# Nine one-hot quads shared between VectorE and ScalarE in the setup, and an earlier codebook request, in a one-core attention and codebook-FFN kernel

## The reference, cut to what matters

```
p = tanh(|phz|) * exp(1j * angle(phz));  prog = p ** arange(L)         # the turns
conv = causal convolution of silu(layernorm(h)) with prog, plus lc * prog * p
Wg, Wu, Wd = codebook[idx_gate], codebook[idx_up], codebook[idx_down]  # dequantized
y = silu(x @ Wg.T) * (x @ Wu.T) @ Wd.T
```

## Time and profile before

| | us |
|---|---|
| three runs: median (lowest to highest) | 1321.85 (1320.96 to 1324.58) |
| the profiled execution, its time | 1320.63 |
| its span in the profile | 1318.8 |
| busy: TensorE, VectorE, ScalarE | 1246.8, 1052.7, 272.3 |
| the setup, up to the first instruction of the attention stage on TensorE | 86.6 |

### The profile page before, as it was taken

One profiled execution on the slowest core, in us unless ns is written; L12 is line 12 of the kernel. 1 busy time (PEld: TensorE's weight loads), 2 busy tenths in 40 slices (PEclk: granted clock), 3 DMA queues, 4 the chain that ended last, 5 costly groups with the idle time before them and its releaser, 6 DMA issues.

```text
span 1318.8 us, 20711 instructions
## 1 busy us (share of the span) xinstructions
PE 1246.8 (95%) x7362; PEld 925.8 (70%) x7362; DVE 1052.7 (80%) x2356; ACT 272.3 (21%) x461; POOL 845.4 (64%) x815
## 2 busy tenths in 40 slices
PE   6868999978999999999999999999999999999988
PEld 4534445434777777777777777777777777789866
DVE  3998888868888778888778888778888778888735
ACT  2326666665101000000000000000001000100115
POOL 3666666666676667776667776666776666777710
PEclk8978999986999999999999999999999999999989
DMA  9222222210333323343323433323433323434203
GB/s 233 34 70 53 47 51 51 51 12 9 91 91 86 75 62 86 88 97 84 76 63 80 97 90 85 73 62 80 92 93 84 68 67 78 97 72 88 52 1 128
DMA packets 94619, 98.79 MB, mean 75 GB/s; under 512 B 48109, under 2 KB 52981, under 8 KB 94518
## 3 DMA queue, kind: packets, MB, share of 16 engines
q1 hardware_dynamic: 64884, 89.16, 22.6%
q0 software_dynamic: 25600, 3.33, 8.5%
q10 hardware_dynamic: 4034, 4.98, 1.3%
HBM read 92.50 MB, written 4.90 MB: 74 GB/s over the span
## 4 chain that ended last, share of the span: by engine, by line
PE 78%; DVE 12%; issue 4%; ACT 3%; POOL 1%; DMA 1%; SPq 1%; POOLq 0%; DVEq 0%; ACTq 0%
PE cand L655 41%; PE bank L655 36%; DVE one_hot L1038 3%; DVE work L1022 2%; DVE work L1286 2%; POOL stage_down L400 1%; DVE chosen L1056 1%; ACT L431 1%; DMA book_in<-in_L_ffn_codebook 1%; PE cand L827 1%; DVE small L1022 1%; DVE h L1248 1%; DVE x L1022 0%; SPq L298 0%; ACT work L431 0%
## 5 line engine op out<-in xcount | busy, mean ns | idle before, releaser
L400 POOL DMA_INDIRECT stage_down<-in_L_ffn_codebook,idx_down x688 | 723.4, 1051 | 350.5 <-issue 168.7
L655 PE MATMUL cand<-one_hot,book 128*128 128x512 f32 (+1 forms) x2592 | 660.4, 397 | 15.3 <-DVE one_hot L1038 15.3
L1038 DVE TENSOR_SCALAR one_hot<-bc,low_of 128x512 fp32r<-128x512 uint16 (+1 forms) x1296 | 541.0, 479 | 98.9 <-PE cand L655 96.0
L655 PEld LDWEIGHTS cand<-one_hot,book 128*128 128x128 f32 x2592 | 485.3, 190 | 146.9 <-DVE one_hot L1038 23.2
L655 PE MATMUL bank<-x1t_hi,w 128*128 128x512 f32 (+1 forms) x704 | 244.4, 403 | 0.0
L1056 DVE SCALAR_TENSOR_TENSOR chosen<-bc,high_of,cand 128x512 f32<-128x512 uint16 (+1 forms) x324 | 234.8, 725 | 3.7 <-PE cand L655 3.7
L387 POOL DMA_INDIRECT stage_gate<-in_L_ffn_codebook,idx_gate x112 | 120.0, 1071 | 61.4 <-issue 25.8
L655 PEld LDWEIGHTS bank<-x1t_hi,w 128*128 128x128 f32 (+1 forms) x704 | 129.9, 186 | 37.0 <-issue 7.3
L655 PE MATMUL bank<-x1t_lo,w 128*128 128x512 f32 (+1 forms) x352 | 141.8, 403 | 0.0
L464 ACT ACTIVATE w<-bank 128x128 fp32r<-128x128 f32 (+1 forms) x88 | 24.0, 273 | 402.7 <-PE bank L655 387.2
L1022 DVE TENSOR_TENSOR x<-x,bank 128x512 f32<-128x512 f32 x84 | 57.3, 682 | 52.5 <-PE bank L655 52.2
(11 more groups left out here) (176 smaller groups left out, 784.6 us busy)
## 6 DMA issues: line engine op xcount, KB each, us to landing
bc<-index_parts SPq DMA_DIRECT2D x292, 256.0 KB, 3.2
stage_down<-in_L_ffn_codebook,idx_down POOLq DMA_INDIRECT x688, 2.7
bc<-index_parts_rest SPq DMA_DIRECT2D x32, 192.0 KB, 3.1
x<-in_L_attn_x ACTq DMA_DIRECT2D x4, 1024.0 KB, 10.9
out_x<-x SPq DMA_DIRECT2D x16, 256.0 KB, 2.0
stage_gate<-in_L_ffn_codebook,idx_gate POOLq DMA_INDIRECT x112, 2.9
index_parts<-parts_t SPq DMA_DIRECT2D x20, 32.0 KB, 2.3
w_in<-in_L_attn_W ACTq DMA_DIRECT2D x2, 256.0 KB
```

The source lines that it names most:

```text
L400: pool.indirect_dma_start(stage_down[k % RING][:, q, j * CS:(j + 1) * CS], None, a["L0_ffn_codebook"], bass.IndirectOffsetOnAxis(ap=idx_do ...
L655: return pe.matmul(dst, lhs, rhs, start=start, stop=stop)
L1038: done = v.tensor_scalar(one_hot[quad % 2][:, q, 0:nw], bc[quad % BCS][:, 0:nw], low_of[:, q:q + 1], None, ALU.is_equal)
```

## The change

- ScalarE makes the third and fourth one-hot tile of quads 0 to 8: `Abs(low - column)` and then `Relu(1 - that)`. VectorE makes the first and second. `candidates` waits for ScalarE's tiles only ahead of the third matmul.
- The conversion of the index parts of tiles 1 to 10 to float, and the four `mix` matrices, go from VectorE to ScalarE.
- `unit` runs after every third doubling only.
- On SP's queue, the codebook's two requests stand ahead of `parts_out(0)`; on VectorE, the wait for the codebook and its split stand ahead of the wait for the turned rows of parameters.

```diff
             # sync
-            parts_out(0)
             for half in range(2):
                 sp.dma_start(book_in[...], ...).then_inc(s["book_in"], 16)
+            parts_out(0)
             for quad in range(BCS):
                 spread_parts(quad)
             # scalar
+            def hots(quad):
+                place = one_hot[quad % 2]
+                act.wait_ge(s[f"bc_in{quad % BCS}"], 16 * (quad // BCS + 1))
+                if quad >= 2:
+                    act.wait_ge(s["candidates"], quad - 1)
+                for n in range(2):
+                    act.activation(place[:, LT - 2 + n, :], bc[quad % BCS][:, 0:4 * P], ACT.Abs, bias=less_low[:, n:n + 1]
+                                   ).then_inc(s["distance_made"], 1)
+                for n in range(2):
+                    act.wait_ge(s["distance_made"], 2 * quad + n + 1)
+                    act.activation(place[:, LT - 2 + n, :], place[:, LT - 2 + n, :].bitcast(F32), ACT.Relu, bias=one[:, 0:1], scale=-1.0
+                                   ).then_inc(s["act_hot_made"], 1)
...
             act.activation(small[:, 8, :], small[:, 7, :], ACT.Sqrt).then_inc(s["phase_sqrt"], 1)
+            act.wait_ge(s["hot_biases"], 2)
+            hots(0)
             act.wait_ge(s["b1_made"], 1)
             keep_h(0, bank[2])
+            hots(1)
             for t, b in ((4, 0), (5, 1), (6, 2), (7, 0)):
                 keep_x(t, bank[b])
             keep_h(1, bank[1])
+            for l in range(L):
+                done = act.activation(mix[:, l, :], centre[:, :], ACT.Copy, scale=cols[:, l, SC_LIN:SC_LIN + 1])
+            done.then_inc(s["mix_made"], 1)
+            hots(2)
             act.wait_ge(s["mag_made"], 1)
             act.activation(cols[:, :, DECAY], small[:, 9, :], ACT.Tanh).then_inc(s["phase_tanh"], 1)
             for t, b in ((8, 2), (9, 0), (10, 1), (11, 2)):
                 keep_x(t, bank[b])
             keep_h(2, bank[0])
+            hots(3)
             for t, b in ((12, 1), (13, 2), (14, 0), (15, 1)):
                 keep_x(t, bank[b])
             keep_h(3, bank[2])
+            act.wait_ge(s["idx_cut"], 2)
+            act.activation(idx_low[:, 1:TILES, :], low_i[:, 1:TILES, :], ACT.Copy)
+            act.activation(idx_high[:, 1:TILES, :], high_i[:, 1:TILES, :], ACT.Copy).then_inc(s["idx_split"], 1)
+            hots(4)
             act.wait_ge(s["eps_made"], 1)
             square1(0)
             for k in range(1, TILES):
                 keep_parts(k, bank[(k - 1) % 3])
                 if k == 5:
                     keep_picked(0)
+                if k in (2, 4, 8):
+                    hots({2: 5, 4: 6, 8: 7}[k])
+            hots(EARLY)
             # tensor, in candidates(quad)
+                        if quad <= EARLY and m == 0 and q >= LT - 2:
+                            pe.wait_ge(s["act_hot_made"], 2 * quad + q - (LT - 2) + 1)
             # vector
-                for q in range(LT):
+                for q in range(LT - 2 if quad <= EARLY else LT):
...
+            v.memset(one[:, :], 1.0).then_inc(s["hot_biases"], 1)
+            v.tensor_scalar(less_low[:, :], iota_low[:, LT - 2:LT], -1.0, None, ALU.mult).then_inc(s["hot_biases"], 1)
...
+            v.wait_ge(s["book_in"], 32)          # with the split of the codebook, moved up from behind b1_made
+            for q in range(LT):
+                link(v.tensor_copy(book[0]...)); tt(book[1]..., ALU.subtract)
             v.wait_ge(s["rows_turned"], 1)
...
-                unit(k + 1, S[10], S[11])
+                if k % 3 == 2:
+                    unit(k + 1, S[10], S[11])
...
-            v.tensor_copy(idx_low[:, 1:TILES, :], low_i[:, 1:TILES, :])
-            v.tensor_copy(idx_high[:, 1:TILES, :], high_i[:, 1:TILES, :]).then_inc(s["idx_split"], 1)
...
-                v.tensor_scalar(mix[:, l, :], centre[:, :], cols[:, l, SC_LIN:SC_LIN + 1], None, ALU.mult)
```

More of the change, by code:

```diff
@@ L171, in build @@
         high_of = sb("high_of", [P, 1])
+        less_low = sb("less_low", [P, 2])
+        one = sb("one", [P, 1])
         one_hot = [sb(f"one_hot{b}", [P, LT, 4 * P], F32R) for b in range(2)]
@@ L253, in build @@
         sem_names = """consts_made masks_made iotas_made eps_made means_made centre_made
-            first_index_in index_in index_down_in index_gate_in idx_cleared first_split idx_split rows_in x_in0 x_in1 x_in2 x_in3 w_in bout_in book_in
+            first_index_in index_in index_down_in index_gate_in idx_cleared first_split idx_cut idx_split rows_in x_in0 x_in1 x_in2 x_in3 w_in bout_in book_in
             parts_turned parts_kept parts_out0 parts_out1 parts_out2 turned_x x_kept turned_w w_kept rows_turned cols_made sums_made b1_made bout_sum bout_made
-            h_sum h_begun phase_sqrt phase_tanh q_made mag_made link layer_made book_made
+            h_sum h_begun phase_sqrt phase_tanh q_made mag_made link mix_made layer_made book_made
             sq1_made var1 rs1_made normed1 silu_made turned_back scanned damped rotated state_kept mixed h_mid
@@ L259, in build @@
             attn_out x_added stats_made aggregated rstd_made shift_made x1_made x1_turned x1_hi x1_lo
-            bc_in0 bc_in1 bc_in2 bc_in3 bc_in4 one_hot_made candidates chosen_made summed picked_hi picked_lo
+            bc_in0 bc_in1 bc_in2 bc_in3 bc_in4 hot_biases distance_made act_hot_made one_hot_made candidates chosen_made summed picked_hi picked_lo
             gate_in down_in0 down_in1 down_in2 turned_down w_hi w_lo gate_made up_made gate_silu product act_hi_made act_lo_made
@@ L817, in _ @@
             pe.wait_ge(s["layer_made"], 1)
+            pe.wait_ge(s["mix_made"], 1)
             pe.wait_ge(s["means_made"], 1)
@@ L1083, in _ @@
             v.tensor_copy(high_of[:, :], iota_m[:, :])
+            v.wait_ge(s["book_in"], 32)
+            for q in range(LT):
+                link(v.tensor_copy(book[0][:, q, :].rearrange("p (e h) -> p h e", e=CS), book_in[:, :, q, :]))
+                tt(book[1][:, q, :].rearrange("p (e h) -> p h e", e=CS), book_in[:, :, q, :],
+                   book[0][:, q, :].rearrange("p (e h) -> p h e", e=CS).bitcast(F32), ALU.subtract).then_inc(s["book_made"], 1)
             v.wait_ge(s["rows_turned"], 1)
@@ L1113, in _ @@
             done.then_inc(s["b1_made"], 1)
[L1114 to L1118, removed]
             one_hots(0)
@@ L1155, in double @@
                     tt(tabq[:, :, new], ta, tb, ALU.add)
+                squared = (S[10], S[11]) if k % 3 == 2 else (cosp[:, :, k + 1], sinp[:, :, k + 1])
                 tt(S[0], cosp[:, :, k], cosp[:, :, k], ALU.mult)
                 tt(S[1], sinp[:, :, k], sinp[:, :, k], ALU.mult)
-                link(v.scalar_tensor_tensor(S[11], cosp[:, :, k], 2.0, sinp[:, :, k], ALU.mult, ALU.mult))
-                link(tt(S[10], S[0], S[1], ALU.subtract))
-                unit(k + 1, S[10], S[11])
+                link(v.scalar_tensor_tensor(squared[1], cosp[:, :, k], 2.0, sinp[:, :, k], ALU.mult, ALU.mult))
+                link(tt(squared[0], S[0], S[1], ALU.subtract))
+                if k % 3 == 2:
+                    unit(k + 1, S[10], S[11])
             double(0)
@@ L1166, in _ @@
             v.wait_ge(s["index_in"], 64)
-            link(v.tensor_scalar(by_quad(low_i, 1, TILES), strided(raw, 1, TILES), LOW - 1, None, ALU.bitwise_and))
-            v.tensor_copy(idx_low[:, 1:TILES, :], low_i[:, 1:TILES, :])
-            link(v.tensor_scalar(by_quad(high_i, 1, TILES), strided(raw, 1, TILES), LOW.bit_length() - 1, None, ALU.logical_shift_right))
-            v.tensor_copy(idx_high[:, 1:TILES, :], high_i[:, 1:TILES, :]).then_inc(s["idx_split"], 1)
+            v.tensor_scalar(by_quad(low_i, 1, TILES), strided(raw, 1, TILES), LOW - 1, None, ALU.bitwise_and).then_inc(s["idx_cut"], 1)
+            v.tensor_scalar(by_quad(high_i, 1, TILES), strided(raw, 1, TILES), LOW.bit_length() - 1, None, ALU.logical_shift_right
+                            ).then_inc(s["idx_cut"], 1)
             double(2)
```

## The result

The changed kernel took 1335.9 us, median of 6 runs (1331.57 to 1339.37), against 1321.08 for the one before (6 runs, 1319.97 to 1324.58): 14.8 us more, a ratio of 1.012 (95% interval 1.0101 to 1.014). The forecast was 1334, slower.

What follows compares the result with a forecast made beforehand. VectorE looked like the bound, but queue order and handovers decide: late parameters, ScalarE's pieces and late broadcasts move the opening root from 89.4 to 102.3, +12.9 on 1320.6, 1333.5 profiled, median 1334; range 1325 to 1341.

Steps and rivals of the forecast that it cites:

- The codebook: SP's queue: requested 1.3 us earlier, landing 0 to 1.3 sooner, taken as 0.6, at 25.0; `bc` 0 at 29.5 to 30.
- The late parameters: VectorE takes the parameter rows only after the codebook's split, 27.4; `h_in(0)` starts at 32.6, first turns of x 8.5 us later.
- ScalarE's pieces: One-hot pieces 2.45 us a quad, both casts 2.45, four `mix` 1.1; ScalarE gets 25.6 us for VectorE's 9.9.
- The clock: TensorE's `h_in(2)`, its candidates and the next round's follow gaps over 3 us: 0.5 us added a round for lower clock.
- The tiles: Index tiles: first `keep_parts` at 74.4; behind SP's output issues `bc` 7 lands 87.9, `bc` 8 97.9; root ends 102.3.
- Setup and total: Opening root ends at 102.3 against 89.4, +12.9; nothing later takes the shift back; median forecast 1334.
- VectorE's relief is the gain: First rival: VectorE was the bound and ScalarE's share hides wholly; gain of some 6 us, 1316; 7 in 100.
- the gains and losses cancel: Second rival: codebook 1.3 sooner, pieces 2.06, no lower clock, tiles and `bc` issued sooner: 1324 to 1326; 10 in 100.
- the third rival: ScalarE costs more: pieces at 3.3 us a quad, +7, or half clock in rounds two to four, some 4; 15 in 100.
- Table loads: ScalarE: one 1.28 us load counted, after `hots(8)`, without the 1.38 drain; abs and relu outside active tables: up to nine more.

Runs made afterwards that it cites:

- second profile: Another profiled execution of the changed kernel, with a span of 1333.7 us; the first profiled execution took 1339.37.
- experiment 1: Changed kernel with the codebook's wait and split back behind `b1_made` on VectorE, SP's order staying changed: 1374.16 us, ratio 1.0072 to the kernel before.
- sixth: Changed kernel with the codebook's part undone on both SP and VectorE, all else as changed: 1326.99 us, ratio 1.0066 to the kernel before.
- seventh experiment: Kernel before with only the rarer renormalization (`unit` after every third doubling): 1317.8 us against 1319.12, ratio 0.999.
- second group: Group of follow-up runs with the kernel before on the same chip: kernel before 1319.12 us, changed kernel again 1334.69.

## Why the prediction was right, step by step

| step | before | forecast | changed | codebook undone |
|---|---|---|---|---|
| `h_in(0)` starts | 22.22 | 32.6 | 33.83 | 22.45 |
| `h_in(1)` | 34.42 | 43.3 | 44.31 | 35.24 |
| `h_in(2)` | 42.58 | 54.8 | 56.21 | 46.90 |
| `h_in(3)` | 50.73 | 64.1 | 67.38 | 58.52 |
| first tile kept | 56.55 | 74.4 | 77.00 | 68.13 |
| opening root ends | 89.4 | 102.3 | 106.3 | 97.0 |

VectorE's first scan in the attention stage, before and after, for the step behind the setup:

```profile
92.88 1.28 DVE L1286 TENSOR_TENSOR_SCAN work<-cols,work 128x512 f32<-128x512 f32 x1
```

```profile
109.14 1.28 DVE L1326 TENSOR_TENSOR_SCAN work<-cols,work 128x512 f32<-128x512 f32 x1
```

- **The codebook.** It landed at 25.2, and the forecast said 25.0: of 1.3 us sooner in the queue 0.4 arrived, and in the second profile (25.62 against 25.61) nothing. SP came back at 21.0, not 19.8, `bc` was asked for at 26.05 and was there by 30.44, hidden as forecast.
- **The late parameters.** The mechanism was right and is confirmed by undoing it (7.7 us in time, 9.2 at the root; this takes back SP's order too). From the rows to `h_in(0)` it took 6.0 us, not 5.2: after ten idle microseconds TensorE's granted clock was 0.50 at 22 to 30 us, and the stretch with its many narrow matmuls took 1.1 us longer than before, where I had added 0.3.
- **ScalarE's pieces.** 2.45 us a quad, 1.26 a cast and 1.27 for four `mix` were forecast within 0.2 us. That the one-hot pieces lose in the rounds is shown by leaving them out (about 7 us at the root).
- **The clock**, the term that was too small. I had 0.5 us in each of two rounds; it was 2.3 in one and nothing in the other. That it is the clock, and that it fell in the 3.2 us gap ahead of the turn (0.51 at 54 to 56 us), is shown by filling this gap, which brought the 2.3 back. Shorter gaps can go either way: the fourth round's, 0.5 and 0.8 us, left the projection at 3.70, those of 0.8 and 2.0 us in experiment 1 stood before one of 5.40.
- **The tiles.** From the first kept tile to the root I had 27.9 us, it took 29.3: `bc` of quad 7 landed 3.7 us after its issue where I had 3.4, and from its landing to the end of tile 10 it took 6.0 us (90.93 to 96.88) where I had 5.3: the candidates of quad 7, 4.1 us long at a granted clock of 0.50, ended 2.6 us behind ScalarE's pieces where I had 2.1.
- **Setup and total.** The setup was lengthened by 16.9 us, 4.0 more than the sum. The medians differ by 14.8, so some 2 us came back later, where I had seen nothing that would take the shift back. The scans of the attention stage, one in each of its 16 items, show how it goes on. The first of them is 16.3 us late (92.88 before, 109.14 after), so 0.6 us came back at once, and all 16 are 16.2 to 16.3 late, in the second profile 16.3 to 16.4: the stage hands the shift through. The second profile was 15.9 us late at the first candidates beside the FFN (337.12 against 321.22) and 14.9 at the end. The first was 17.7 late there and 18.8 at the end, so executions of the same kernel part behind the attention stage, and what takes or gives there stays open. The closeness of 1334 to 1335.9 owes something to luck: two errors of opposite sign, 4.0 too little in the setup and some 2 us that came back.
- **The rivals.** That VectorE's relief is the gain falls with the sixth and seventh experiment: even alone on the kernel before, 5.8 us less work gave 2.1 at the root and, in time, nothing that the interval tells from zero. That the gains and losses cancel did not occur. Of the third rival a part did: one `h_in` at the lower clock, not three, and pieces at the price that I had taken.
- **Table loads.** On ScalarE the load ahead of the root begins 0.01 us after the piece before it (102.94 + 1.32, 104.27), and the root 0.02 us after the load (105.57): no drain of the kind that the Trainium skill, "ScalarE: Activation LUTs", section "What ACT_TABLE_LOAD costs", states is to be seen. The prediction says that it counted one load, but its walk has a second one on the path, with the Tanh up to 52.8. Two drains of the page's 1.38 us would have made the sum +15.7, an estimate that is nearer to the measured 16.9 than mine, yet the rows leave no room for the second either: pieces until 52.35, load at 52.37, Tanh at 53.67. The rule of the same page, section "Table sets: the hidden batching unit", that abs and relu are in every set agrees: ScalarE has 503 instructions after and 461 before, and the 42 more are 36 pieces, 2 casts and 4 `mix`, with no load among them (44 loads in both).

## What to carry to other kernels

An engine that is mostly idle (ScalarE was busy for 21% of the span) can still be the wrong place for work, if each of its idle stretches lies inside a round of handovers: ask between which two instructions the new one will stand, and who waits for the second. A wait put at the head of an in-order queue delays everything behind it, ready or not; a request for data that is last through a full set of DMA engines gains little by being made sooner (here 0 to 0.4 us of 1.3). Work that is freed on one engine counts only up to the next thing that this engine waits for, so look for that before adding up what was removed.

## What the runs showed of the hardware

An activation of 128x512 with a bias column costs 0.61 us in a row whether it reads 16-bit or 32-bit data from SBUF (two in 1.33, four in 2.45). A gap of 3.2 us on TensorE cost 2.3 us in the projection behind it, and four matmuls in the gap that nobody needed avoided it: the busier engine was done sooner. Six executions of the changed kernel spread over 7.8 us (1331.6 to 1339.4) and six of the kernel before over 4.6; in the second group it was 1.8 and 7.6 (19 runs of the kernel before), so the spread is no mark of the change, and what makes it stays open.
